# A recurrence and a mixture of experts on one core: x on two queues ahead of longer projections, and sorted rows turned by transposing DMAs

## The reference

```python
def _L0_cond_ref(x, h0, Wx, Wh, b):
    xp = jnp.einsum('ntd,dh->nth', x, Wx) + b
    def step(prev_h, xp_t):
        next_h = jnp.tanh(xp_t + prev_h @ Wh)
        return (next_h, next_h)
    _, h = jax.lax.scan(step, h0, jnp.swapaxes(xp, 0, 1))
    return jnp.swapaxes(h, 0, 1)

def _L0_ffn_ref(x, shared_w1, shared_w2, experts_w1, experts_w2, gate_w):
    x_flat = x.reshape(T, D)
    shared = jnp.einsum('td,dh->th', x_flat, shared_w1.T)
    shared = jnp.einsum('th,hd->td', jax.nn.silu(shared), shared_w2.T)
    gate_logits = x_flat @ gate_w.T
    top_k_gates, top_k_idx = jax.lax.top_k(gate_logits, TOP_K)
    top_k_gates = jax.nn.softmax(top_k_gates, axis=1)
    ...
    h = jnp.einsum('td,ehd->teh', x_flat, experts_w1)
    expert_out = jnp.einsum('teh,edh->ted', jax.nn.silu(h), experts_w2)
    selected = jnp.einsum('ted,te->td', expert_out, gates)
    return (shared + selected).reshape(B, S, D)

x = x + _L0_ffn_ref(_L0_cond_ref(x, cond_1024, ...), ...)
```

## Time and profile before

| | |
|---|---|
| timed runs, median (lowest to highest) | 385.0 us (383.47 to 388.58) |
| profiled execution | 381.38 us |
| its span | 379.7 us |
| TensorE busy | 356.2 us, 94% |
| ScalarE busy | 244.1 us, 64% |
| VectorE busy | 200.2 us, 53% |
| GpSimd busy | 108.5 us, 29% |
| DMA, queue of SyncE | 66.9% of 16 engines' span |
| DMA, queue of GpSimd | 16.9% |

### The profile page before, as it was taken

How to read it: one execution, slowest core, us unless ns; L and a number is a source line. 1 busy time by engine, 2 the same in 40 slices (tenths; PEclk the granted TensorE clock), 3 DMA queues, 4 the chain that set the end, 5 groups by cost and what they waited for, 6 DMA issues and landing times.

```text
span 379.7 us, 8904 instructions
## 1 busy us (share of the span) xinstructions
PE 356.2 (94%) x2458; PEld 253.0 (67%) x2459; DVE 200.2 (53%) x415; ACT 244.1 (64%) x478; POOL 108.5 (29%) x99
## 2 busy tenths in 40 slices
PE   5989999997997998999999999999999999999981
PEld 4758889964664675666667666667766666666660
DVE  0089999979996988964333323333323333232310
ACT  3777788888556778865555665556665556665530
POOL 1100010000276788600123333223333133332241
PEclk9999999999999999999999999999999999999996
DMA  6999999607697979999898998889988989989992
GB/s 194 422 421 434 428 407 334 194 4 124 87 199 182 225 180 226 235 194 196 176 129 153 168 155 155 147 149 156 158 149 154 148 142 158 148 159 147 152 127 28
DMA packets 158173, 73.50 MB, mean 194 GB/s; under 512 B 140736, under 2 KB 155200, under 8 KB 156992
## 3 DMA queue, kind: packets, MB, share of 16 engines
q1 hardware_dynamic: 146672, 59.83, 66.9%
q0 software_dynamic: 6864, 9.11, 16.9%
q10 hardware_dynamic: 4608, 4.20, 4.1%
HBM read 23.68 MB, written 16.53 MB: 106 GB/s over the span
## 4 chain that ended last, share of the span: by engine, by line
PE 80%; ACT 6%; DMA 5%; issue 3%; DVE 2%; another core or an unknown queue 1%; ACTq 1%; POOL 0%; SPq 0%; DVEq 0%; POOLq 0%
PE py L1138 32%; PE z L1033 30%; PE z L1047 8%; PE z L982 3%; PE z L1014 3%; DMA space<-recurrence_w 2%; DMA space<-space 2%; ACT space L799 1%; ACT space L876 1%; PE px L1025 1%; PE py L982 1%; PE z L995 1%; DMA space<-x_cols 1%; ACTq L896 1%
## 5 line engine op out<-in xcount | busy, mean ns | idle before, releaser
L1138 PE MATMUL py<-w_slots,space 128*128 (+1 forms) x1272 | 148.4, 273 | 7.4 <-DMA space<-recurrence_w 3.7
L1033 PE MATMUL z<-w_slots,x 128*128 (+1 forms) x636 | 145.9, 379 | 0.8 <-issue 0.8
L1138 PEld LDWEIGHTS py<-w_slots,space 128*128 128x128 f16 x1272 | 123.8, 98 | 33.1 <-issue 3.5
L1033 PEld LDWEIGHTS z<-w_slots,x 128*128 128x128 f16 x636 | 62.1, 98 | 65.0 <-issue 1.2
L453 POOL DMA_INDIRECT out<-space x37 | 57.5, 1553 | 157.0 <-issue 65.2
L876 ACT ACTIVATE space<-z,tile_scales 128x512 f32<-128x512 f32 x106 | 71.8, 678 | 41.3 <-PE z L1033 34.1
L582 DVE SCALAR_TENSOR_TENSOR recurrence_w<-space,tile_scales,recurrence_w 128x512 f16<-128x512 f32 x54 | 40.5, 750 | 71.7 <-ACT recurrence_w L881 65.6
L582 DVE SCALAR_TENSOR_TENSOR space<-space,tile_scales 128x512 f16<-128x512 f32 x52 | 39.0, 750 | 57.7 <-ACT space L881 42.4
L528 DVE SCALAR_TENSOR_TENSOR w_slots<-w_slots,w_scale 128x1024 f16<-128x1024 f32 x36 | 46.2, 1283 | 1.3 <-issue 0.3
L881 ACT ACTIVATE recurrence_w<-space,tile_scales 128x512 f16<-128x512 f32 x54 | 39.0, 722 | 8.7 <-ACT space L876 2.5
L430 POOL DMA_INDIRECT sorted_rows<-space x32 | 39.1, 1221 | 17.5 <-issue 13.1
(11 more groups left out here) (114 smaller groups left out, 178.9 us busy)
## 6 DMA issues: line engine op xcount, KB each, us to landing
w_slots<-weights SPq DMA_DIRECT2D x9, 2048.0 KB, 30.5
sorted_rows<-pad_row SPq DMA_DIRECT2D x1, 5070.0 KB, 60.2
space<-x_rows ACTq DMA_DIRECT2D x16, 128.0 KB
out<-space ACTq DMA_DIRECT2D x16, 128.0 KB
space<-x_cols SPq DMA_DIRECT2D x1, 1024.0 KB, 8.6
space<-recurrence_w SPq DMA_TRANSPOSE x54
space<-space SPq DMA_TRANSPOSE x52
x<-sorted_rows SPq DMA_TRANSPOSE x39
```

The costliest lines, as they stand in the source:

```text
L1033: last = nc.tensor.matmul(Z[u % 2][h][:], x16[:, u, x_part, k], weight(f, k * HID + h * BANK, BANK, part), start=k == 0 and x_part == 0 an ...
L1138: last = nc.tensor.matmul(PY[p][:, 0:D], hiddenT[:, p, low, q], weight(f, MATRIX + q * D, D, part), start=q == 0 and not low and part == 0 ...
```

## The change

Front: SyncE issues x first and loads it in five parts, with the first network's weights in two halves between them; ScalarE's queue carries Wx, h0 and the bias. TensorE begins with six products of a constant tile. The projections run two blocks ahead of the guess steps, behind the step in TensorE's order, and ScalarE's copy of a projection stands behind the tanh. The last tanh of a round writes the next round's start itself, so the copies `next_start` on ScalarE and the semaphore `start_ok` go. VectorE searches 14 chunks in place of 16, and the shared network's scale is found by itself, in a batch of its own, before the second network is searched. ScalarE searches from chunk 14 on; five searches instead of four lie behind the rounds, one right after them and one in each of the tiles 1 to 4, and the last reduction follows those. The unrolled loops lose their hardware loop.

Sort: `rows`, `sort_row` and `row_low` go. SyncE turns tile t of `x16` into `hr` (`turn_row`) by a transposing DMA of 512 columns, in the order of `ROWS_AT`. The states' float16 pair is made three tiles ahead in place of two (`STATES_AT`), and ScalarE waits for the turned row before it overwrites a place of the ring. A late weight split moves from later tiles to tile 5 (`SPLITS_AT`).

```diff
-ARRIVALS = ((0, 1), (1, 2), (2, 4), (4, BLOCKS))
+ARRIVALS = ((0, 1), (1, 2), (2, 4), (4, 6), (6, BLOCKS))
...
+WARM_UP = 6
+ROWS_AT = {0: (0, 1, 2), 1: (3,), 3: (4, 5), 4: (6, 7), **{t - 3: (t,) for t in range(8, TILES)}}
+STATES_AT = {0: (2, 3), **{t - 3: (t,) for t in range(4, TILES)}}
+EARLY_WIDES = 22
+BOUND_BATCHES = ((0, 1), (1, 2), (2, 3), (3, 4), (4, 5), (5, 6), (6, FFNS))
+FOUND_BY_DVE = 2 * CHUNKS - 2
+LATE_FINDS = (FFNS * CHUNKS - LATE_FINDS_FROM) // 2
+SPLITS_AT = {3: (22, 23), 5: (24,), 6: (25, 26), 7: (27,), 8: (28, 29), 9: (30,), 10: (31,), 11: (32, 33), 12: (34,), 13: (35,)}
...
         def _(sp):
+            load_x(0)
+            sp.dma_start(wh_sb, wh).then_inc(wh_in, 16)
+            load_x(1)
+            load_x(2)
+            load_weights(0, 0, CHUNKS // 2, w_up_in)
+            load_x(3)
+            load_weights(0, CHUNKS // 2, CHUNKS, w_in[0])
+            load_x(4)
...
+            def turn_row(t):
+                sp.wait_ge(x_lo_ok, t + 1)
+                if t == RING:
+                    sp.wait_ge(routed, 1)
+                if t >= SORT_RING:
+                    sp.wait_ge(sorted_ok[t % SORT_RING], 16 * TOP)
+                sp.dma_start_transpose(hr16[:, t % SORT_RING, 0:2 * D].rearrange("p (a n) -> p a n", n=P),
+                                       x16[:, t % RING].rearrange("p a k n -> p (a k n)")).then_inc(row_in[t % RING], 16)
             for g in range(TILES):
                 turn(g, g % 2)
+                for t in ROWS_AT.get(g, ()):
+                    turn_row(t)
...
         def _(pool):
-                if n == 0:
-                    pool.wait_ge(bound_ok, 2)
-                else:
+                if n < 2:
+                    pool.wait_ge(bound_ok, n + 2)
+                if n > 0:
                     pool.wait_ge(found, found_upto(end))
...
-                waited(row_ok, t + 1)
+                waited(row_in[t % RING], 16 * (t // RING + 1))
...
         def _(act):
+            nc.scalar.dma_start(wx_sb, wx).then_inc(wx_in, 16)
+            nc.scalar.dma_start(states[:, :, 0, 0:B], h0_cols).then_inc(h0_in, 16)
+            nc.scalar.dma_start(bias_sb[:], bias).then_inc(bias_in, 16)
...
-            for m in range(K):
-                project_out(0, m)
+            for n in range(K + 1):
+                project_out(n // K, n % K)
             for i in range(BLOCKS):
                 for u in range(2):
-                    if i + 1 < BLOCKS:
-                        project_out(i + 1, u)
                     for m in range(K):
                         act.wait_ge(z_mm[m], i * 2 + (u + 1))
...
+                    n = i * K + u + K + 1
+                    if n < BLOCKS * K:
+                        project_out(n // K, n % K)
...
-                if g + AHEAD < TILES:
-                    shared_rows(g + AHEAD, x_hi_ok)
-                elif g + 1 == TILES:
+                for t in STATES_AT.get(g, ()):
+                    act.wait_ge(row_in[t % RING], 16 * (t // RING))
+                    shared_rows(t, x_hi_ok)
...
-                if sorting:
-                    sort_row(row)
                 hidden_half(g, g % 2, n, 1)
-                if sorting:
-                    sort_row(row + 1)
-                if g <= WIDES // 2:
+                if g < LATE_FINDS:
+                    find_last(g)
...
         def _(pe):
+            pe.wait_ge(consts, 1)
+            for _ in range(WARM_UP):
+                nc.tensor.matmul(PX1[:, 0:P], ones[:], ones[:], start=True, stop=True)
             pe.wait_ge(wx_in, 16)
...
-            for m in range(K):
-                project(0, m)
+            for n in range(2 * K):
+                project(n // K, n % K)
             pe.wait_ge(guess_ok, 3)
             for i in range(BLOCKS):
                 for u in range(2):
-                    if i + 1 < BLOCKS:
-                        project(i + 1, u)
                     guess_step(i, u)
+                    if i + 2 < BLOCKS:
+                        project(i + 2, u)
...
-                if sorting:
-                    rows(2 * (g - SORT_FROM))
```

More of the change, by code:

```diff
@@ L54 @@
 ROW = D + META
+ROW_PITCH = ROW + 4
 SORT_RING = 8
@@ L1141, in down @@
                 last.then_inc(down_mm, 1)
-            def rows(t):
-                if t >= 2:
-                    pe.wait_ge(row_ok, t - 1)
-                for k in range(K):
-                    last = nc.tensor.transpose(row_bank[t % 2][:, k * P:(k + 1) * P], states[:, k, t + 1], identity[:])
-                last.then_inc(row_mm, 1)
             def expert(t):
```

184 lines of the change are left out of this document (72 added, 112 removed).

## The result

The changed kernel takes 388.7 us (median of 20 runs, 384.07 to 392.46), the kernel before 384.2 us beside it (20 runs, 381.63 to 390.18). The ratio is 1.0097, 95% interval [1.0072, 1.0122]: about 1% slower, where 0.3% faster was forecast. Within 2%, but the sign was wrong. The ratio leaves out the slowest runs of both kernels (over 1.5% above the fastest), so it is smaller than that of the two medians.

What follows compares the result with a forecast made beforehand. The sort on GpSimd was taken to bound tile 16: front's 2.8 us lost at ScalarE's new wait, transposes' 8.8 us mostly swallowed waiting for the sort, leaving 385.0 - 1.1 = 383.9 us, range 376.5 to 390.

Steps and rivals of the forecast that it cites:

- the sort: GpSimd's 32 row scatters before tile 16: 52.5 of 56.4 us stay, so they bound the time; gain 1.1 us.
- Start: GpSimd's first scatter, behind the last reduction of bounds: at 109.0 us, 5.7 us later than before.
- Pace: GpSimd's scatters in the sort: their own 39.1 us plus 0.30 us or more of issue between them stay.
- R1: Rival: GpSimd and the sort get faster, tile 16 near 162, 8 us gained, 377; over 4 us gained, chance 0.30.
- Completion: End of the sort: last scatter begins at 160.1 us, lands 4.6 us later, complete at 164.7.
- TensorE's own stretch: TensorE before tile 16 without transposes: tile 16 at 162.2 us, 8.8 us earlier, if nothing else stopped it.
- R2: Rival: DMA engines decide, 9 us slower, 394; chance of being slower at all 0.22, of nearly the full price 0.07.
- step (d): Second exact round: TensorE's work, gain nothing; VectorE's weight splits start earlier and so follow.
- (a): First product at the front: x awaited until 3.9 us, first guess step at 8.0 in place of 8.6, gain 0.6.
- (b): Guess steps at the front: 1.14 us each, eight pairs save 0.19 each, 1.5 us.
- New wait: ScalarE in tile 1 waits for row 0's DMA: 4.8 us (3.4 to 5.5), down 1 at 97.1, front's gain lost.
- the case of being slower at all: The whole kernel slower than before by any amount, from the DMA engines deciding; chance 0.22.

Runs made afterwards that it cites:

- e9: The changed kernel unaltered, traced again on another chip; 381.67 us, ratio 1.0103 to the kernel before.
- e8: The changed kernel with GpSimd's last reduction of bounds queued behind the scatters of rows 0 and 1; 382.4 us, ratio 1.007.
- e4: The changed kernel unaltered, for a second profile; 384.69 us in one run.
- e10: The changed kernel with rows 8 to 15 turned two or three tiles earlier, from other tiles' places in the ring; 381.41 us, ratio 1.0047.
- e6: The changed kernel with VectorE's search of the second weights moved ahead of its wait for GpSimd's first reduction; 381.04 us, ratio 1.003.
- e11: The changed kernel with two repairs, the edits of e6 and e8 together; 380.61 us, ratio 1.0022.
- e15: The changed kernel with all three repairs, the edits of e6, e8 and e14; 380.77 us, ratio 0.9923.
- e12: The change's front alone (e1) with the two edits of e11, rows turned by TensorE as before; 376.23 us, ratio 0.9932.
- e14: The changed kernel with tile 4's copy made in tile 2 in place of tile 1, the third repair alone; 389.59 us, ratio 1.0098.
- e1: The changed kernel with the old row code put back, so the change's front alone; 384.85 us, ratio 1.0061.
- e3: The changed kernel with each row copied by a plain DMA of the same size, not turned; 384.02 us, ratio 1.0043.
- e7: The changed kernel with GpSimd's first reduction queued ahead of its masks and counts; 383.98 us, ratio 1.0099.
- e2: The kernel before with only the rows turned by DMA, its front unchanged; 391.32 us, ratio 1.0217.
- e16: The kernel of e15 with rows 8 to 15 turned two or three tiles earlier, from earlier tiles' places; 381.46 us, ratio 0.9894.
- e18: The kernel of e2 again, unaltered, on the chip of e6 to e8; 391.41 us, ratio 1.0212.

## Why the prediction was wrong

The step that failed was the sort: "52.5 stay, the scatters' own 39.1 and the 0.30 us or more of issue between them". The forecast took GpSimd's pace for its own and the last row for as early as GpSimd wanted it. It had the sort as the bound, which e9 confirms, but its end wrong: last scatter at 160.1 forecast and 164.25 in e9, tile 16 at 168.5 and 171.24, down 14 at 172.4 and 174.00, where before has 173.55. Its own last sentence had named the risk: "I'd be most wrong if GpSimd's pace in the sort were not its own."

- **Start.** Forecast 109.0, measured 111.2 (110.5 in e9). It matters little: e8.
- **Pace.** The scatters take 35.2 us in place of 39.1, and the first half comes 5.4 us faster. R1's premise held. But R1's 8 us didn't come, since from row 8 on row t is turned only in tile t - 3, and 8.2, 4.3 and 4.0 us of waiting replaced the gain. Had I followed row 15 back (turn 12, tile 12's copy, the ring of four) I'd have seen that no pace of GpSimd helps it: the last scatter begins 9.7 us after turn 12's issue in e4, 10.0 in after (163.8 to 173.83), 11.7 in e9.
- **Completion.** 164.7 forecast for the rows sorted, 4.6 us behind the start of the last scatter. In e9 they are sorted 2.7 us behind it, by 167.0; in the other traces the landing takes up to 5.3 (e8). So the landing hid part of the miss of 4.1 us at the last scatter, which is luck. In after the last scatter is at 173.83, tile 16 at 179.81, because the issue gaps had moved every tile and with it every row.
- **TensorE's own stretch.** "If nothing else stopped it, twelve tiles of 5.21 us": the idle 4.5 us of before did not go. e9 has 3.8 us of idle time between 100 and 150, now mostly at turns of hidden rows, and 2.9 us more at tile 16. Of the 8.8 us nothing is left. This may be R2's road at a small size. Windows don't stop growing at 1.17, and the earlier trace rows was not even the fullest of before; the first line is before's, the second e9's:

```profile
125.00:130.00 5.00, 5.00 (x36) 3.31 (x33) 4.93 (x8) 3.55 (x7) 4.52 (x4) 1.00 1.24 225
133.00:138.00 5.00, 5.00 (x36) 3.42 (x35) 4.93 (x8) 4.30 (x7) 4.22 (x6) 1.00 1.22 289
```

  Neither has any idle time of TensorE, so the share of a window told nothing of when the engines are full. Whether the turns come late by a row's 1.2 us of issue between them in SyncE's queue or by its 0.65 us of load is open.
- **Issue gaps.** No step had them. They and the lower clock are why after's profile is 10 us behind: 12.9 us by the estimate above, of which part only takes the place of e9's waits. Before has 0.7 and 0.2 us of them in two traces. With them (the result) and without (e9) the ratio is 1.01.
- **Front, step (d)**, "it follows": wrong. VectorE stood for GpSimd, and of 2.8 us forecast at the first SiLU 0.2 came (between -1.5 and 1.0 in the other traces with this front, e4, e8, e9 and e10). Moving one search into the wait puts it at 82.08, and e6's ratio is 1.003 where e8's is 1.007. (a) was wrong by 0.6, and by 2.3 to 3.4 us in the six traces with slow projections; (b) was right in its 1.14 us a step.
- **New wait.** Right: 5.21 us (4.8 forecast, 3.4 to 5.5), the row landing 3.5 us after its issue, down 1 at 98.87 (97.1), 1.8 late by the front's missing gain. Taken away alone it gave nothing, with the others the ratio went from 1.0022 (e11) to 0.9923 (e15), on different chips, so what it costs by itself is not shown.
- **Range and chances.** 388.7 lies in 376.5 to 390 and the time is within 2%, the likeliest case, but by the width of the range and not by the mechanism: the case of being slower at all, given 0.22, is the one that came.

What wins is not the transposes' new engine: e12 (TensorE turns the rows) and e15 (DMA does, with one repair more) end at 0.9932 and 0.9923 on different chips, their intervals one on the other. What the repairs are worth is shown on one chip each: the first two take the change from 1.0103 (e9) to 1.0022 (e11), and on top of the third from 1.0098 (e14) to 0.9923 (e15), with intervals apart both times, though e14's trace has 8.9 us of gaps and e15's 1.5. So the gain is likely the front's with its waits repaired; e1, the front without the repairs, has 1.0061, with 4.3 us of gaps where e12 has none. By the Trainium skill's table of the three transpose paths (VectorE: DVE Perf Modes) DMA is more than three times as slow for a block. No run here times one block; a row of four landed in 2.5 to 4.1 us in e9, below the prediction's estimate of 5.2.

## What to carry to other kernels

When a step moves from one engine to a DMA, follow its last instance back: through the buffer it reads, to the stage that fills it, and through the queue it stands in. A sort that needs all rows ends with the last, however fast the scatters are. And an input that comes earlier gains nothing until the first operation of each helper engine has been looked up in the trace, since a start-up may be what is late next (6.7 to 13.0 us for GpSimd here).

## What the runs showed of the hardware

- Ahead of GpSimd's first reduction over partitions, where it follows the masks and counts, stand 6.7 (e9) to 8.9 us (e3) that the profile gives to no wait. With the reduction first (e7) the counts stand 10.2 us and the next reduction 10.5. Ahead of the first mask it is 7.8 us before and 13.0 after, while the loads run. A pair of `MODIFY_POOL_CONFIG` records stands near the head of each such time: at 1.6 and 16.0 us in after, at 1.6, 17.8 and 29.1 in e7. That they are the cause is likely, not tested.
- A transposing DMA of a row, on-chip to on-chip, lands 2.5 to 4.1 us after its issue in e9 (median 3.9), up to 6.9 in e8, and takes 1.26 us of the issuing queue; the two of a turn take 2.6 at the least, up to 5.4 in e8 and 6.8 in e12, which has no rows.
- TensorE can run its products in pieces, with 0.2 to 1.7 us between them and no wait that the profile shows, in traces where GpSimd issues indirect DMAs without a pause. The granted clock is 0.50 for a while in after, e2, e14, e16 and e18 (5.0 to 8.9 us of gaps), and stays at 1.00 in e1 with 4.3 us.
- An indirect DMA of GpSimd that ends the sort lands 2.7 us (e9) to 5.3 us (e8) behind its start.
- The time around the span is 2.1 us in the change and 1.7 in before, e1 and e2: 0.4 us of the profiled loss lies outside the trace.
